# Attention and ternary FFN on one core: scores made twice instead of transposing p, and one written schedule of 64 heads

## The chip, the cores and the metric

The kernel runs on one core of a Trainium2 chip. The metric is the device time of one execution, in microseconds (us). The kernel before takes 694.51 us, the median of three runs (694.48 to 696.26).

PE is the tensor engine (PEld its weight loads), DVE the vector engine, ACT the scalar engine, POOL GpSimd, SP the engine that issues most DMAs. Each runs its own program in order, and they meet by semaphores.

## The reference, cut to what matters

```python
# x: (4, 512, 512) f32; 16 query heads of 32, one key and one value head
q = rotary((x @ Wq + bq).reshape(4, 512, 16, 32).transpose(0, 2, 1, 3))
k = rotary((x @ Wk + bk)[:, None])
v = (x @ Wv + bv)[:, None]
scores = einsum('bhqd,bhkd->bhqk', q, k) / sqrt(32)
attn = softmax(scores, axis=-1)
ctx = einsum('bhqk,bhkd->bhqd', attn, v)            # -> (4, 512, 512)
x = layernorm(x + ctx @ Wo + bo)
# FFN: w1, w2 (1408, 512), w3 (512, 1408); ternary weights
qz = lambda w: clip(round(w / (mean(abs(w)) + 1e-8)), -1, 1)
hidden = sigmoid(x @ qz(w1).T) * (x @ qz(w2).T)
out = layernorm(x + hidden @ qz(w3).T)
```

## The kernel before, in words

Four batches of 512 tokens are worked one after another. A batch has 16 heads, in four groups of four. Queries are projected per group (a unit, `q0` to `q3`, f32 products, eight instructions), keys once (unit `k`). A unit is copied out of its bank by ACT into `raw`, rotated by POOL (times cosine) and DVE (shuffle, times sine, sum), and split into a high and a low half in the matmul's reduced f32 type, `hi` and `lo`. SP then stacks the four heads of a unit into `q_st` by 16 small DMAs (`stack`), high and low on different partitions, so that one product of 128 rows gives a score of f32 quality against `k_st`.

For each head and each tile t of 128 queries:

1. `score` (PE, L935): one product 128x128 by 512 keys into a ring of three banks `s_ps`, in the first batch four.
2. `row_max` (DVE, L697): the minimum of the negated scores, straight from the bank.
3. `exps` (ACT, L458): the exponential with that shift as bias; `accum_out` sums the row. p stands by query.
4. `turn` (PE, L947): 16 transposes of 128x128 per head bring p to stand by key, into two banks `t_ps`; ACT and DVE each `move` two of the four tiles to `pt_sb` (L468, L703).
5. After four heads, `context` (PE, L997): the values' 32 columns against `pt_sb`, the heads in four column strips of the array, each k tile of each head two instructions. The reciprocals of the sums are spread and turned (`reciprocals`, `turn_sums`, `norm_row`), and DVE multiplies (`normalise`).

Beside the heads of batch b runs the output projection (`wo0` to `wo3`), the layer norm, the turning of h (`ht`) and the FFN (`up`, 11 tiles of two halves, `dn0` to `dn3`) of batch b - 1, in banks `a_ps` and `b_ps`, placed by a list:

```python
BESIDE = (["up0", "up1", "up2", "up3", "q2", "up4", "up5", "up6", "q3"]
          + [f"up{f}" for f in range(7, FT)] + ["dn0", "dn1", "dn2", "dn3"])
```

wo and ht stand ahead of the batch's heads, with `q0`, `k` and `q1`. The first batch has heads only (`first_heads`), and there ACT sums the absolute weights, DVE rounds w1 and w3 (`quantise`) and POOL w2 (`round_w2`). Batches 1 to 3 are one loop body of each engine. After it comes a tail: wo, ht, up and dn of batch 3 alone. The order of each engine's work is written out by hand in `first_heads`, `heads` and `period`; no planner is used.

## Time and profile before

| | |
|---|---|
| median of the runs | 694.51 us |
| the profiled execution | 694.24 us |
| its span, first to last instruction | 692.4 us |
| PE busy | 634.5 us (92%) |
| DVE busy | 491.6 us (71%) |
| ACT busy | 353.3 us (51%) |
| POOL busy | 93.1 us (13%) |
| mean granted clock of PE | 0.968 |

Busy PE is not PE at its peak: products are pipelined and their shown ends overlap the next start. How long one takes in a row of many is read from the distance of starts. The profile's page names lines of the kernel before (L955 is `turn`, L944 `score`, L916 `up`, L930 `dn`, L882 a query unit, L903 `wo`, L1008 `context`, L962 the key and value parts, L893 `ht`).

### The profile page before, as it was taken

How to read it: one execution, taken by the hardware profiler on the slowest of the kernel's cores; microseconds unless marked ns; L12 is line 12 of the kernel's file. 1: busy time of each engine (PE TensorE's matmuls, PEld its weight loads, DVE VectorE, ACT ScalarE, POOL GpSimd, SP SyncE). 2: the span in 40 equal slices, each digit the busy share in tenths (PEclk: the TensorE clock that was granted, in tenths of full speed). 3: DMA queues.
4: the chain of work that ended last, by engine and by line, in shares of the span. 5: the costliest groups of instructions: out<-in, count | busy, mean ns of one | idle time of the engine just before them, and what ended most of it. 6: DMA issues, size and time to landing. Idle time of an engine off the chain costs nothing.

```text
span 692.4 us, 10936 instructions
## 1 busy us (share of the span) xinstructions
PE 634.5 (92%) x3342; PEld 347.6 (50%) x3342; DVE 491.6 (71%) x833; ACT 353.3 (51%) x814; POOL 93.1 (13%) x118
## 2 busy tenths in 40 slices
PE   6777577699999999999999999999999999998996
PEld 2544345434556565634556565534556564543442
DVE  2879967947887985758887985658878985554333
ACT  2795576522676585412677685312767675302320
POOL 1000562012000400121000400122000400110001
PEclk9799789799999999999999999999999999999999
DMA  7662450001132040021122030011122110000001
GB/s 268 228 204 62 167 162 22 1 16 46 29 95 62 9 114 3 16 65 46 43 85 58 23 101 2 25 61 41 47 88 51 29 34 2 31 30 1 0 1 61
DMA packets 20516, 42.03 MB, mean 61 GB/s; under 512 B 4704, under 2 KB 5856, under 8 KB 19936
## 3 DMA queue, kind: packets, MB, share of 16 engines
q1 hardware_dynamic: 19488, 39.86, 19.0%
q10 hardware_dynamic: 960, 1.33, 0.5%
q8 instruction: 34, 0.56, 0.3%
q14 instruction: 34, 0.28, 0.1%
HBM read 20.20 MB, written 4.19 MB: 35 GB/s over the span
## 4 chain that ended last, share of the span: by engine, by line
PE 74%; DVE 11%; issue 6%; ACT 3%; DMA 3%; SPq 1%; POOL 1%; DVEq 0%; POOLq 0%; ACTq 0%
PE t_ps L955 14%; PE a_ps L916 11%; PE b_ps L916 10%; PE c_ps L1008 8%; PE a_ps L882 7%; PE s_ps L944 6%; PE a_ps L930 6%; PE b_ps L930 6%; PE a_ps L903 3%; DVE sh_sb L700 3%; DMA late<-in_w 2%; PE b_ps L903 2%; DVE pt_sb L707 1%; SPq L286 1%; PE a_ps L993 1%
## 5 line engine op out<-in xcount | busy, mean ns | idle before, releaser
L464 ACT ACTIVATE p_sb<-s_ps,sh_sb 128x512 f32<-128x512 f32 x240 | 164.4, 689 | 106.9 <-DVE sh_sb L700 106.9
L955 PE MATMUL t_ps<-table_sb,p_sb 128*128 128x128 f32 x1024 | 143.5, 284 | 26.4 <-ACT pt_sb L472 23.7
L700 DVE TENSOR_REDUCE sh_sb<-s_ps 128x1 f32<-128x512 f32 x240 | 157.6, 679 | 0.8 <-PE s_ps L944 0.7
L955 PEld LDWEIGHTS t_ps<-table_sb,p_sb 128*128 128x128 f32 x1024 | 123.0, 146 | 67.0 <-ACT p_sb L464 33.3
L707 DVE COPY pt_sb<-t_ps 128x512 f32<-128x512 f32 x128 | 88.1, 688 | 69.3 <-PE t_ps L955 67.5
L472 ACT ACTIVATE pt_sb<-t_ps 128x512 f32<-128x512 f32 x128 | 76.5, 597 | 51.4 <-PE t_ps L955 49.6
L944 PE MATMUL s_ps<-k_st,q_st 128*128 128x512 f32 x240 | 91.0, 463 | 4.0 <-DVE k_st L627 2.5
L916 PE MATMUL a_ps<-late,q 128*128 128x512 f16 x352 | 85.2, 386 | 3.5 <-DVE late L642 3.4
L916 PE MATMUL b_ps<-late,q 128*128 128x512 f16 x352 | 83.6, 380 | 0.0
L882 PE MATMUL a_ps<-xT_sb,wq_sb 128*128 128x512 f32 x128 | 61.8, 614 | 8.7 <-DMA wq_sb<-in_wq 6.4
L361 POOL TENSOR_TENSOR rot<-raw,table_sb 128x512 f32<-128x512 f32 x20 | 25.9, 1295 | 306.6 <-ACT raw L433 291.6
L1008 PE MATMUL c_ps<-pt_sb,v_sb 128*32 128x512 f32 x512 | 59.5, 606 | 2.1 <-DVE pt_sb L707 2.1
L916 PEld LDWEIGHTS a_ps<-late,q 128*128 128x128 f16 x352 | 32.0, 99 | 46.9 <-issue 8.2
L916 PEld LDWEIGHTS b_ps<-late,q 128*128 128x128 f16 x352 | 31.9, 98 | 39.4 <-issue 5.4
L944 PEld LDWEIGHTS s_ps<-k_st,q_st 128*128 128x128 f32 x240 | 43.1, 200 | 12.1 <-ACT p_sb L464 5.8
L464 ACT ACTIVATION_READ_ACCUMULATOR p_sb<-s_ps,sh_sb 128x1 f32 x240 | 48.3, 201 | 0.0
L377 POOL TENSOR_SCALAR rstd<-mv 128x1 f32<-128x1 f32 x32 | 8.4, 263 | 278.0 <-DVE mv L670 277.9
L930 PE MATMUL b_ps<-q,late 128*128 128x512 f16 x176 | 41.3, 380 | 0.0
L903 PE MATMUL a_ps<-wo_sb,cx 128*128 128x512 f32 x88 | 40.2, 599 | 0.5 <-DVE late L690 0.4
L930 PE MATMUL a_ps<-q,late 128*128 128x512 f16 x176 | 40.4, 380 | 0.0
L882 PEld LDWEIGHTS a_ps<-xT_sb,wq_sb 128*128 128x128 f32 x128 | 23.3, 195 | 33.0 <-issue 23.9
L657 DVE SCALAR_TENSOR_TENSOR b_ps<-th,b_ps 128x512 f32<-128x512 f32 x33 | 23.0, 696 | 22.6 <-PE b_ps L916 20.5
(82 smaller groups left out, 602.2 us busy)
## 6 DMA issues: line engine op xcount, KB each, us to landing
q_st<-hi SPq DMA_DIRECT2D x128, 64.0 KB, 2.0
q_st<-lo SPq DMA_DIRECT2D x128, 64.0 KB, 2.0
late<-in_w SPq DMA_DIRECT2D x2, 2816.0 KB, 11.3
xT_sb<-in_xT SPq DMA_DIRECT2D x8, 512.0 KB, 4.9
late<-in_x SPq DMA_DIRECT2D x4, 1024.0 KB, 5.6
out<-late SPq DMA_DIRECT2D x16, 256.0 KB, 2.0
late<-in_w SPq DMA_DIRECT2D x2, 1408.0 KB, 6.9
wo_sb<-in_wo SPq DMA_DIRECT2D x1, 1024.0 KB, 5.6
```

Of the source, the lines that this page charges most:

```text
L361: pool.tensor_tensor(rot[:, 0, :], raw[:, u % 2, :], cos_sb, ALU.mult).then_inc(cos_done, 1)
L464: act.activation(p_sb[:, h % 2, t, :], score_bank(b, n), ACT.Exp, bias=sh_sb[:, n % (2 * SR):n % (2 * SR) + 1], scale=-1.0, accum_out=sums ...
L472: act.activation(pt_sb[:, h % PTR, k, :], t_ps[k % 2][:, :], ACT.Copy).then_inc(pt_act, 1)
L700: dve.tensor_reduce(sh_sb[:, n % (2 * SR):n % (2 * SR) + 1], score_bank(b, n), AX.X, ALU.min).then_inc(maxed, 1)
L707: dve.tensor_copy(pt_sb[:, h % PTR, k, :], t_ps[k % 2][:, :]).then_inc(pt_dve, 1)
L882: mm = pe.matmul(a_ps[:, :], wq_sb[:, k, g * P:(g + 1) * P], xT_sb[:, k, :], start=(k == 0), stop=(k == DT - 1))
L903: mm = pe.matmul(ps[:, :], cx[:, g, t * P:(t + 1) * P], wo_sb[:, g, :], start=(g == 0), stop=(g == HG - 1))
L916: mm = pe.matmul(ps[:, :], w[:, k, f * P:(f + 1) * P], hT[:, s, k, :], start=(k == 0 and s == 0), stop=(k == DT - 1 and s == 1))
L930: mm = pe.matmul(ps[:, :], gT[:, s, f, t * P:(t + 1) * P], q3v[:, f, :], start=(f == 0 and s == 0), stop=(f == FT - 1 and s == 1))
L944: pe.matmul(score_bank(b, n), q_st[:, h % (QR * HPG), t * P:(t + 1) * P], k_st[:, :], start=True, stop=True).then_inc(scored, 1)
L955: mm = pe.transpose(t_ps[k % 2][:, t * P:(t + 1) * P], p_sb[:, h % 2, t, k * P:(k + 1) * P], id_sb)
L1008: mm = pe.matmul(c_ps[HD * j:HD * (j + 1), :], v_sb[:, k, :], pt_sb[:, (g * HPG + j) % PTR, k, :], start=(k == 0), stop=(k == TT - 1))
```

## The change

The scores are made twice. `rows` is the old `score`, used only for the maximum of each query; `cols` takes `k_st` as the weights and `q_st` as the moving side, so the scores stand by key. In front of a group of four heads DVE spreads the maxima (high and low part, `spread_maxima`), PE turns them (`turn_maxima`), ACT copies them to `mrow`, and four `pick` products per head, 32 rows of the array each, subtract the query's maximum inside the bank. ACT's exponential then writes `pt_sb` directly, without bias and without a row sum. The 16 transposes of p per head, their moves and `p_sb` are gone.

The sums of p over the keys are made by PE with a matrix of ones: for the first two groups (DIRECT) from the four k tiles of p, later from `acc`, into which POOL has added the four tiles (`add_keys`, three additions per head). DVE inverts them with its own transposes of 32x32 (`inverse_sums`).

Banks: four `t_ps`, one for each k tile of `cols`; `a`, `b`; `c` for key, value and context; `r` for `rows`, the turned maxima and the sums. Up to head 21 the `rows` alternate between `r` and `b`, after it all are in `r`.

All three steps of a rotation are on POOL, and so is all rounding of weights. ACT waits, before it copies the key or value parts of the next batch into `lo`, until all four units of the batch have been stacked. The order is one list of slots, one slot a head, straight through all 64 heads, with no loop body; `rows` run four heads ahead of `cols`, and every engine follows the same `order`. wo, ht, up of batch b - 1 start at slot 3, its last two down tiles stand in slots 1 and 2 of batch b + 1. The first units are made key first.

```diff
-PTR = HPG
-PIECES = 8
-W2_PIECES = 4
-SR = 3
-UNITS = ["q0", "k", "q1", "q2", "q3"]
+N = B * H
+PTR = HPG + 1
+PIECES = 4
+DIRECT = 2
+TWO_BANKS = 22
+UNITS = ["k", "q0", "q1", "q2", "q3"]
+BESIDE = [
+    ["ctx3a", "ctx3b", "q2a", "q2b"],
+    ["sums3", "dn2a", "dn2b", "dn2c"],
+    ["dn3a", "dn3b", "dn3c"],
+    ["wo0a", "wo0b", "wo1a", "wo1b"],
+    ["ctx0a", "ctx0b", "wo2a", "wo2b"],
+    ["sums0", "wo3a", "wo3b", "q3a", "q3b"],
+    ["ht0", "ht1", "ht2", "ht3"],
+    ["up0a", "kp", "up0b", "key", "up1a"],
+    ["vp", "up1b", "val", "up2a", "ctx1a", "ctx1b"],
+    ["sums1", "up2b", "up3a", "up3b", "q0a"],
+    ["q0b", "up4a", "up4b", "up5a"],
+    ["up5b", "up6a", "up6b", "up7a"],
+    ["ctx2a", "ctx2b", "up7b", "up8a"],
+    ["sums2", "up8b", "q1a", "q1b", "up9a"],
+    ["up9b", "up10a", "up10b", "dn0a"],
+    ["dn0b", "dn0c", "dn1a", "dn1b", "dn1c"],
+]
+FIRST = [
+    ["q2a", "q2b"], ["tot0"], [], [],
+    ["ctx0a", "ctx0b", "sums0"], ["tot1", "q3a", "q3b"], [], ["kp", "key", "vp", "val"],
+    ["ctx1a", "ctx1b", "sums1"], ["q0a", "q0b"], [], [],
+    ["ctx2a", "ctx2b"], ["sums2", "q1a", "q1b"], ["tot2"], [],
+]
+OPENING = ["kp", "q0a", "q0b", "key", "vp", "q1a", "val", "q1b"]
...
+def order(b, h):
+    if b >= B:
+        return chunks(b, h)
+    beside, names = chunks(b, h), []
+    if h % HPG == 0:
+        names += ["turn"] + beside[:1]
+        beside = beside[1:]
+    names += ["cols"]
+    for t in range(TT):
+        if b * H + h + HPG < N:
+            names += [f"rows{t}"]
+        names += beside[t:t + 1]
+    return names + beside[TT:]
+def row_bank(n, t):
+    return "rb"[t % 2] if n < TWO_BANKS else "r"
...
 @block.sync
+            def stack(b, g):
+                sp.wait_ge(hi_done, unit(b, f"q{g}") + 1)
+                for j in range(HPG):
+                    n = b * H + g * HPG + j
+                    if n >= QR * HPG:
+                        sp.wait_ge(cols_filled, n - QR * HPG + 1)
+                    for r in (0, 2, 1, 3):
+                        half = (hi, lo)[r % 2]
+                        if j == 0 and r == 1:
+                            sp.wait_ge(lo_done, unit(b, f"q{g}") + 1)
+                        sp.dma_start(q_st[HD * r:HD * (r + 1), ring(n), :].bitcast(F32),
+                                     half[HD * j:HD * (j + 1), :].bitcast(F32)).then_inc(q_in[j], 16)
+            for b in range(B):
+                if b >= 2:
+                    store(b - 2, 0)
+                    store(b - 2, 1)
+                stack(b, 2)
+                if b >= 2:
+                    store(b - 2, 2)
+                    store(b - 2, 3)
+                if b + 1 < B:
+                    load_xT(b + 1)
+                stack(b, 3)
+                if b == 0:
+                    sp.wait_ge(rounded, PIECES)
+                    sp.dma_start(stage[2], w3).then_inc(w_ffn[2], 16)
+                load_x(b)
+                if b + 1 < B:
+                    stack(b + 1, 0)
+                    stack(b + 1, 1)
+            for c in (B - 2, B - 1):
+                for t in range(TT):
...
 @block.gpsimd
+            def rotate(b, name):
+                u = unit(b, name)
+                where = "c" if name == "k" else "a"
+                pool.wait_ge(drained[where], at("key" if name == "k" else name, b))
+                pool.wait_ge(rotated, u)
+                pool.tensor_tensor(rot[:, 0, :], raw[:, :], cos_sb, ALU.mult).then_inc(cos_done, 1)
+                pool.wait_ge(swapped, u + 1)
+                pool.tensor_tensor(rot[:, 1, :], rot[:, 1, :], sin_sb, ALU.mult).then_inc(sin_done, 1)
+                pool.wait_ge(sin_done, u + 1)
+                pool.wait_ge(cos_done, u + 1)
+                pool.tensor_tensor(rot[:, 1, :], rot[:, 0, :], rot[:, 1, :], ALU.add).then_inc(rotated, 1)
+            def add_keys(n, step):
+                j, p, done = n % HPG, n % PTR, 3 * (n - DIRECT * HPG)
+                if step == 0 and n // HPG > DIRECT:
+                    pool.wait_ge(filled["r"], at(f"sums{(n // HPG - 1) % HG}", (n // HPG - 1) // HG))
+                pool.wait_ge(expd, n * TT + step + 2)
+                if step:
+                    pool.wait_ge(added, done + step)
+                pool.tensor_tensor(acc[:, j, :], acc[:, j, :] if step else pt_sb[:, p, 0, :],
+                                   pt_sb[:, p, step + 1, :], ALU.add).then_inc(added, 1)
...
 @block.scalar
+            def take_parts(b, name):
+                act.wait_ge(filled["c"], at(name, b))
+                for j in range(HPG):
+                    act.wait_ge(q_in[j], b * HG * 16 * 4)
+                act.activation(part[:, :], c_ps[:, :], ACT.Copy).then_inc(drained["c"], 1)
+            def take_maxima(gg):
+                act.wait_ge(filled["r"], at("turn", gg, "r"))
+                act.activation(mrow[:, :], r_ps[:, :], ACT.Copy).then_inc(drained["r"], 1)
+            def exps(n, k):
+                act.wait_ge(cols_filled, n + 1)
+                if k == 0 and n >= PTR:
+                    old = n - PTR
+                    gg = old // HPG
+                    act.wait_ge(filled["c"], at(f"ctx{gg % HG}", gg // HG))
+                    if gg < DIRECT:
+                        act.wait_ge(filled["r"], at(f"sums{gg % HG}", gg // HG))
+                    else:
+                        act.wait_ge(added, 3 * (old - DIRECT * HPG + 1))
+                act.activation(pt_sb[:, n % PTR, k, :], t_ps[k][:, :], ACT.Exp).then_inc(expd, 1)
...
 @block.vector
+            def row_max(n, t):
+                where = row_bank(n, t)
+                dve.wait_ge(filled[where], at(f"rows{t}", n, where))
+                dve.tensor_reduce(mx[:, t, n % HPG:n % HPG + 1], banks[where][:, :], AX.X,
+                                  ALU.max).then_inc(drained[where], 1)
+            def spread_maxima(gg):
+                last = gg * HPG + HPG - 1
+                for t in (TT - 2, TT - 1):
+                    where = row_bank(last, t)
+                    dve.wait_ge(drained[where], at(f"rows{t}", last, where))
+                if gg == 0:
+                    dve.wait_ge(turned_set, 1)
+                else:
+                    dve.wait_ge(filled["r"], at("turn", gg - 1, "r"))
+                every = mx[:, :, :].unsqueeze(2).broadcast_to([P, TT, HPG, HPG])
+                dve.tensor_copy(maxima[:, :, :, 0:HPG], every).then_inc(max_hi, 1)
+                dve.wait_ge(max_hi, gg + 1)
+                dve.tensor_tensor(maxima[:, :, :, HPG:2 * HPG], every, maxima[:, :, :, 0:HPG].bitcast(F32),
+                                  ALU.subtract).then_inc(max_done, 1)
+            def inverse_sums(gg):
+                name, b = f"sums{gg % HG}", gg // HG
+                dve.wait_ge(filled["r"], at(name, b))
+                dve.tensor_reduce(sm[:, :], r_ps[:, :].rearrange("p (m r) -> p m r", r=HD), AX.X, ALU.max,
+                                  apply_transpose=True).then_inc(drained["r"], 1)
+                dve.wait_ge(drained["r"], at(name, b))
+                dve.reciprocal(rc[:, :], sm[:, :]).then_inc(recip_done, 1)
+                dve.wait_ge(recip_done, gg + 1)
+                dve.transpose(rT.rearrange("p (m r) -> p m r", r=HD),
+                              rc[:, :].unsqueeze(2).broadcast_to([P, TT * HPG, HD])).then_inc(rT_done, 1)
+            def follow(b, name):
+                if name[:2] == "up" and name[-1] == "b":
+                    g_low(batch_of(b, name), int(name[2:-1]))
+                elif name[:4] == "sums":
+                    normalise(batch_of(b, name) * HG + int(name[4]))
+            def end(b, name):
+                if name[:2] == "wo" and name[-1] == "b":
+                    norm(batch_of(b, name), 0, int(name[2]))
+                elif name[:2] == "dn" and name[-1] == "c":
+                    norm(batch_of(b, name), 1, int(name[2]))
+                for name in order(b, h):
+                    chunk(b, h, name)
+                    follow(*gone[-1])
+                    end(*gone[-3])
+                    stack_halves(*gone[-5])
+                    gone.append((b, name))
...
 @block.tensor
+            def rows(n, t):
+                b, h = divmod(n, H)
+                where = row_bank(n, t)
+                ps = start_bank(f"rows{t}", n, where)
+                if t == 0:
+                    pe.wait_ge(q_in[n % HPG], (n // HPG + 1) * 16 * 4)
+                if t == 0 and h == 0:
+                    pe.wait_ge(lo_done, unit(b, "k") + 1)
+                pe.matmul(ps[:, :], q_st[:, ring(n), t * P:(t + 1) * P], k_st[:, b % 2, :],
+                          start=True, stop=True).then_inc(filled[where], 1)
+            def turn_maxima(gg):
+                start_bank("turn", gg, "r")
+                pe.wait_ge(max_done, gg + 1)
+                for t in range(TT):
+                    mm = pe.transpose(r_ps[:, t * P:(t + 1) * P], turned[:, t, :].bitcast(F32), id_sb)
+                mm.then_inc(filled["r"], 1)
+            def cols(n):
+                b, j = n // H, n % HPG
+                if n == 0:
+                    pe.wait_ge(pick_set, 1)
+                if j == 0:
+                    pe.wait_ge(drained["r"], at("turn", n // HPG, "r"))
+                for k in range(TT):
+                    if n:
+                        pe.wait_ge(expd, (n - 1) * TT + k + 1)
+                    pe.matmul(t_ps[k][:, :], k_st[:, b % 2, k * P:(k + 1) * P], q_st[:, ring(n), :],
+                              start=True, stop=False)
+                for k in range(TT):
+                    mm = pe.matmul(t_ps[k][:, :], pick[HD * k:HD * (k + 1), j, :], mrow[HD * k:HD * (k + 1), :],
+                                   start=False, stop=True)
+                mm.then_inc(cols_filled, 1)
+            def sums(gg):
+                start_bank(f"sums{gg % HG}", gg // HG)
+                if gg < DIRECT:
+                    pe.wait_ge(expd, (gg + 1) * HPG * TT)
+                    for k in range(TT):
+                        for j in range(HPG):
+                            mm = pe.matmul(r_ps[HD * j:HD * (j + 1), :], ones[:, 0:HD],
+                                           pt_sb[:, (gg * HPG + j) % PTR, k, :], start=(k == 0), stop=(k == TT - 1))
+                else:
+                    pe.wait_ge(added, 3 * HPG * (gg - DIRECT + 1))
+                    for j in range(HPG):
+                        mm = pe.matmul(r_ps[HD * j:HD * (j + 1), :], ones[:, 0:HD], acc[:, j, :],
+                                       start=True, stop=True)
+                mm.then_inc(filled["r"], 1)
```

## Rows read from the trace of the kernel before

**Rows 1.** Stretches: us; PE, PEld, DVE, ACT, POOL busy; granted clock, DMA share, GB/s.

```profile
21.80:144.57 122.77, 88.84 (x487) 57.78 (x487) 100.49 (x167) 80.72 (x190) 25.74 (x18) 0.85 0.35 115
...
456.80:607.60 150.80, 149.61 (x829) 82.30 (x828) 113.28 (x193) 83.98 (x197) 17.82 (x23) 1.00 0.15 42
607.60:692.40 84.80, 75.08 (x313) 33.78 (x311) 36.46 (x64) 15.88 (x26) 7.66 (x18) 0.96 0.05 19
```

**Rows 2.** Timeline of PE, a head beside an up tile: start, us, instruction.

```profile
337.96 0.93 PE L944 MATMUL s_ps<-k_st,q_st 128*128 128x512 f32 x3
338.74 1.90 PE L916 MATMUL a_ps<-late,q 128*128 128x512 f16 x8
340.48 1.04 PE L955 MATMUL t_ps<-table_sb,p_sb 128*128 128x128 f32 x8
341.27 0.50 PE L944 MATMUL s_ps<-k_st,q_st 128*128 128x512 f32 x1
341.62 1.90 PE L916 MATMUL b_ps<-late,q 128*128 128x512 f16 x8
```

**Rows 3.** Timeline of PE, key parts and what follows.

```profile
148.20 1.06 PE L962 MATMUL c_ps<-xT_sb,small_sb 128*32 128x512 f32 x8
149.19 3.70 PE L903 MATMUL a_ps<-wo_sb,cx 128*128 128x512 f32 x8
```

**Rows 4.** Groups by line: count, busy us, mean ns, idle before and its releaser.

```profile
L700 DVE TENSOR_REDUCE sh_sb<-s_ps 128x1 f32<-128x512 f32 x240 | 157.6, 679 | 0.8 <-PE s_ps L944 0.7
...
L707 DVE COPY pt_sb<-t_ps 128x512 f32<-128x512 f32 x128 | 88.1, 688 | 69.3 <-PE t_ps L955 67.5
L472 ACT ACTIVATE pt_sb<-t_ps 128x512 f32<-128x512 f32 x128 | 76.5, 597 | 51.4 <-PE t_ps L955 49.6
```

**Rows 5.** Timeline: a lone score and its row maximum, and a last DVE step of ht.

```profile
484.37 0.58 PE L944 MATMUL s_ps<-k_st,q_st 128*128 128x512 f32 x1
...
485.17 0.68 DVE L700 TENSOR_REDUCE sh_sb<-s_ps 128x1 f32<-128x512 f32 x1
...
626.81 0.69 DVE L642 SCALAR_TENSOR_TENSOR late<-b_ps,late 128x512 f16<-128x512 f32 x1 [0.30 <-ACT late L440]
```

**Rows 6.** Timeline of the opening: stacking, splitting and rotating.

```profile
15.89 1.23 SPq L286 DMA_DIRECT2D q_st<-hi  x2
...
18.37 0.69 DVE L617 TENSOR_TENSOR rot<-rot 128x512 f32<-128x512 f32 x1
...
19.09 0.42 DVE L624 CAST k_st<-rot 64x512 fp32r<-64x512 f32 x1
19.35 1.28 POOL L361 TENSOR_TENSOR rot<-raw,table_sb 128x512 f32<-128x512 f32 x1 [1.62 <-ACT raw L433]
19.54 1.37 DVE L625 CAST k_st<-rot 64x512 fp32r<-64x512 f32 x1
```

**Rows 7.** The chain that ended last, in order of time: w2's load, a context.

```profile
26.66 13.15 DMA late<-in_w
...
235.10 3.57 PE c_ps L1008 x32
```

**Rows 8.** Waits from 22 to 144.57: us in total, times, longest.

```profile
PE t_ps L955 <- ACT pt_sb L472: 23.7, 15, 3.9
```

**Rows 9.** Waits of PE from 144.57 to 609: us in total, times, longest.

```profile
PE a_ps L882 <- issue: 2.0, 2, 1.3
PE a_ps L916 <- DVE late L642: 2.0, 3, 0.7
PE a_ps L903 <- DVE late L690: 0.4, 2, 0.3
```

**Rows 10.** Timeline of PE in the tail: the last wo to the first up.

```profile
617.89 3.60 PE L903 MATMUL b_ps<-wo_sb,cx 128*128 128x512 f32 x8
621.32 0.60 PE L893 MATMUL a_ps<-table_sb,late 128*128 128x128 f32 x4
...
627.56 3.55 PE L916 MATMUL a_ps<-late,q 128*128 128x512 f16 x8 [1.42 <-DVE late L642]
```

More of the change, by code:

```diff
@@ L1124, in _ @@
[L1124 to L1138 removed]
+                if third == 2:
+                    mm.then_inc(filled[where], 1)
```

1245 lines of the change are left out of this document (466 added, 779 removed).

## The prediction

> **What bounds the kernel now.** I read the table of stretches first. It cuts the span where PE begins a new batch. In the three middle periods (144.57 to 607.60, on average 154.3 us) PE is busy nearly all the time at full clock, DVE about 75% and ACT 56% (here of the last one). In the first batch (21.8 to 144.57) PE is busy 72%, the granted clock falls to 0.85 and a head takes 122.8 / 16 = 7.7 us; DVE is the fullest engine [rows 1]. The timeline of PE in a middle period says how full it really is: the starts of the groups follow each other with no gap, 8 transposes 0.79 us, 3 scores 0.78 (0.26 each), 8 f16 products of 512 columns 1.74, a score alone 0.35 [rows 2]. The longer groups: key parts (four column strips at once) 0.99 [rows 3], a context of four heads 3.57 [rows 7], a four-tile f32 product, eight instructions, 3.43 [rows 10]. Added up over a period (64 scores, 256 transposes, 4 contexts, 11 up pairs, 4 down, 8 f32 products, small ones) this gives about 150 of 154.3 us. So the middle is PE's, by issued work; only in the first batch do the others decide. There the waits say who: PE for ACT's move of the transposed tile, 23.7 us [rows 8].
>
> The chip must therefore be asked two things: does PE get less work per batch, and does the new order keep PE fed.
>
> **PE's work per period.** Removed: 16 transposes per head, two groups of 0.79, so 16 x 1.58 = 25.3 us, and the four turns of sums at 0.4, 1.6 us; together 26.9. Added:
> - `cols`, four scores by key, 4 x 0.26 = 1.05 per head [rows 2]: 16.8.
> - the four `pick` products that add the maximum. Each has 32 rows of the array and 512 columns. No row shows row strips. Upper bound: each costs a score, 4 x 0.26 = 1.05 per head. Lower bound: all four stream as one, 0.26. The nearest row is the key parts, where 8 instructions on four column strips take 0.99, while two instructions of the four-tile product take 3.43 / 4 = 0.86 [rows 3, 10], so strips run together; with four weight loads I take 0.45: 7.2.
> - `rows` is today's score, but now always alone: 48 of them rise from 0.26 to 0.32: 2.9.
> - turning the maxima, 4 x 0.42 (half a group of eight): 1.7; `sums` as four column strips, 4 x 1.0: 4.0.
>
> Added 32.6, net +5.7 us per period. The work that leaves ACT (two moves of 597 ns) and DVE (two moves of 688 ns) [rows 4] is worth nothing here, because PE did not wait for them.
>
> Of the pick products the Trainium skill says more ("TensorE: Matmul & The Clock Gate", section "Measured speedup vs the span model"): four tiles of 32 rows and 512 columns ran 3.07 times as fast as one after another. By that rule a head would pay 1.05 / 3.07 = 0.34 and the period 1.8 us less than in my sum; no row here shows it.
>
> **New waits of PE.** From head 22 on, `rows` has the single bank `r`. A lone score's row maximum starts 0.80 us after the row says the score started (0.6 after it really streams, behind the previous group), the reduction takes 0.68 [rows 4, 5], and PE goes on 0.06 after a DVE end (626.81 + 0.69 against 627.56) [rows 5, 10], say 0.1. So from a `rows` to the next use of `r` about 0.6 + 0.68 + 0.1, 1.35 us, of which 0.3 is its own: PE needs 1.05 us of other work between. Most chunks are halves of 1.72 and hide it, with 0.7 left for one DVE operation ahead in its queue. Where they don't:
> - `sums0` to `sums3` also use `r` and stand directly between `rows0` and `rows1`: 1.05 before, 1.05 after (a reduction again), four times: 8.4.
> - slot 6 puts the four `ht` (0.42 each) between the `rows`. Each has an ACT copy and a DVE subtraction in front of the next row maximum, and ACT has two exponentials first, and the split of q3 stands in DVE's queue. Worked through, the slot takes 6.9 us after `cols` for 2.9 us of work: 4.0.
> - after wo0, wo2, dn3 and dn0 the evacuation with its statistics (1.6 us of DVE) stands before a row maximum: four times 0.7, 2.8.
> - `kp` of the next batch must be copied into `lo`, so ACT waits until SP has issued all 16 copies of q3: 0.63 us each [rows 6], 10.1, which end about 2 us after PE wants `key`: 2.0.
>
> Together 17.2. Today's waits, 4.4 us over three periods [rows 9], may go: -1.5. The period becomes 154.3 + 5.7 + 17.2 - 1.5 = 175.7 us.
>
> Work also moves between stretches. Of what three periods hold today, the new ones lack two down tiles (9.5), one batch's q0, q1 and key and value parts (10.7) and `rows` of four heads (5.1), which stand in front or behind: 3 x 175.7 - 25.3 = 501.8 us against 463.0: +38.8.
>
> **Opening and first batch.** Today the first score stands at 21.8 [rows 1]. Now the order is: key first (its three rotation steps now on POOL at 1.28 each instead of one there and two of 0.69 on DVE [rows 6]), so q0's halves about 27 instead of 15.9; 16 copies at 0.63 and 2.0 landing: 39.6; DVE's q1 split waits for them in front of the maxima of heads 2 and 3, eight at 0.60 follow; turning: first `cols` at 46.
> A bare slot is a loop: `cols` end, 0.25, four exponentials at 0.60 (as long as ACT's move of a bank [rows 4]), the last bank's score 0.26, picks 0.45: 3.6 us, where a head had 7.7. That is the gain of the change: 16 x 3.6 = 57.6. On top comes what stands in one line with it: three contexts 10.7, sums directly from p (two at 3.57, then 1.0) 8.1, four q units 13.7, key and value chunks 3.8, maxima 2, the wait for w2 (its load goes out only after q1's copies, about 50; today it went at 26.66 and took 13.15 [rows 7]) 2. And `kp` at slot 7 meets q3's copies: q3b, 0.9 ACT, 4.0 POOL, 1.1 DVE, 10.1 SP, 2.0 landing, against 7.7 of PE work: 10.7. POOL, with eight roundings of 4.6 us and three additions per head from head 8 on, holds the split of q0 (3) and `sums2` (4.5). Sum 116, end at 162 us, against 144.6 today: +17.4.
> The additions of p for three quarters of the heads are 3 x 1.28 = 3.9 us per head on POOL, under a slot of 10.9; hidden outside this stretch.
>
> **Tail.** Today 84.8 us [rows 1]. New in it: context of the last group 3.6, its sums 1.0 and their wait for POOL 0.7, two down tiles of batch 2, 2 x 4.75, and norm three names after wo, so that ht2 and ht3 come later: today 6.2 us lie between the end of the last wo (621.32) and the first up [rows 10], then about 8.2. Together 16.8, so 101.6. The up pairs stay at 1.73 per product: th now carries the gate too, and the loop gate, g_high, g_low, tanh ends 3.3 us after the product that starts it, just under two products.
>
> **Sum.** 692.4 + 17.4 + 38.8 + 16.8 = 765.4 us of span. The profiled execution took 694.24 with a span of 692.4, 1.8 more, and the median of the runs, 694.51, is 0.3 above it. So 767 us.
>
> **Rivals.**
> - It is faster. Mechanism: neither the bank `r` nor the copies of q3 hold PE, because DVE and ACT have more air than I give them, so the bare loop of 3.6 us per head decides in the first batch. Place: the 17.2 us of waits per period and the 18.2 in the first batch go (51.6 + 18.2), and picks cost 0.34 (7): 767 - 77 = 690. If also the opening, where I let every step wait for the last, is 5 us shorter, 685. It decides once less than about 5 of these 82 us remain, since the sum without them is 9 below today. For it: ACT drops from 51% to a third; DVE rows are short [rows 4]. Against: a `sums` between two `rows` on one bank can't be hidden by idle engines, it is latency. Chance 0.12.
> - The pick products run one after another (no strips by rows): 0.6 more per head, 64 heads, +38: 805 us. For it: no row shows it otherwise. Chance 0.10.
> - DVE and POOL hold each other up. While POOL multiplied at 19.35, a DVE cast that takes 0.42 took 1.37 [rows 6]. POOL now works half of each period instead of an eighth, and g_low reads th and gT in SBUF instead of a bank. Some 34 DVE operations per batch read SBUF (g_low, halves, swap, norm); half of them meet POOL at 0.95 each, 16 us per period, of which half lies in front of a row maximum or a gate: 3 x 8, 791 us. Chance 0.10. By the Trainium skill ("SBUF — State Buffer", section "Who interferes with whom") a DVE operation with two SBUF inputs, or in a two-port mode, and a GpSimd operation that reads SBUF exclude each other for a whole instruction; the row agrees.
> - The gains of the first batch and the losses balance, 692 to 697: 0.03.
>
> **Numbers.** The forecast, 767, has 0.65; its own range is 728 to 800 (first batch 20 either way, waits of a period 6 either way, picks 0.26 to 0.6). Range over the cases: 705 to 803; below lies most of the faster case, above half of the serial picks. A change under 0.3% is what this kernel's measurement can't tell from none. Faster 0.12, same 0.03, slower 0.85.
>
> **What would show it.** The starts of `cols`, pick and `rows` give their spacing: 0.26, 0.45 per four, 0.3. Idle of PE before `sums` and before the `rows1` behind it, 1 us each, released by DVE's row maximum and by the transposing reduction. Slot 6: `rows` released by DVE. First `cols` near 46, b=1 beginning near 162, batch periods near 176, the tail 102. PE's idle before `key`, released by ACT, 10 us in the first batch. I am wrong if PE's idle time in the middle is under 5 us per period, or if the first batch ends before 140.

## The result and the profile after

The changed kernel takes 837.06 us (median of 4 runs, 834.47 to 837.82) against 695.12 for the kernel before on the same chip: ratio 1.202, 95% interval 1.198 to 1.206. It is 142 us slower. The forecast, 767, had the direction right and the size wrong: 837 lies outside the range of 705 to 803.

The page's busy times and its slices (tenths of 40 equal slices) show no full engine:

```profile
PE 683.8 (82%) x3006; PEld 302.5 (36%) x3006; DVE 442.3 (53%) x682; ACT 239.5 (29%) x430; POOL 396.0 (48%) x351
...
PE   5478758768877898888987798988987999987997
...
POOL 2325465798946329255546328255546282531001
PEclk9678969788889899999999999999999999998999
```

The table of stretches of the kernel after, cut at its first `cols`, at the turn of the maxima of each new batch and at the last context (columns as in [rows 1]):

```profile
0.00:51.00 51.00, 28.22 (x66) 11.68 (x67) 19.38 (x33) 7.95 (x12) 12.59 (x16) 0.77 0.49 159
51.00:185.11 134.11, 97.03 (x434) 41.98 (x433) 73.73 (x115) 52.65 (x94) 82.13 (x62) 0.86 0.30 96
185.11:379.17 194.06, 162.93 (x694) 72.05 (x695) 106.43 (x156) 55.35 (x101) 111.40 (x92) 0.91 0.13 35
379.17:567.36 188.19, 160.60 (x739) 72.16 (x738) 112.32 (x168) 55.37 (x101) 93.60 (x83) 0.98 0.14 40
567.36:726.91 159.55, 143.90 (x681) 64.86 (x679) 87.79 (x135) 52.34 (x96) 82.18 (x74) 0.98 0.09 27
726.91:832.70 105.79, 91.09 (x397) 39.80 (x396) 42.64 (x75) 15.88 (x26) 14.07 (x25) 0.94 0.05 20
```

Against [rows 1]: a middle period had 1.2 us of TensorE's idle time, now b=1 and b=2 have 31 and 28. In b=1 the granted clock is 0.91, and TensorE is busy 162.9 us with less work than in b=2, where it is busy 160.6 at 0.98: so its own products take longer there as well. Set beside the forecast the span's 67.3 us too many (832.7 against 765.4) fall so: opening 51.0 for 46 (+5.0), first batch 134.1 for 116 (+18.1), b=1 194.1 for 166.2 (+27.9), b=2 188.2 for 175.7 (+12.5), b=3 159.6 for 159.9 (-0.4), tail 105.8 for 101.6 (+4.2). (The forecast's 166.2 and 159.9 are its 175.7 less the 9.5, and less the 10.7 and 5.1, that it let move out of these batches.)

What TensorE waited for, over the whole span (us in total, times, longest):

```profile
PE r_ps L842 <- DVE mx L631: 56.0, 51, 3.4
PE r_ps L849 <- DVE turned L647: 16.0, 9, 3.5
PE c_ps L825 <- ACT lo L494: 12.1, 3, 9.8
PE r_ps L842 <- DVE sm L653: 10.5, 13, 0.8
PE r_ps L891 <- DVE mx L631: 9.4, 12, 0.8
...
PE b_ps L842 <- DVE mx L631: 6.9, 9, 1.7
PE r_ps L891 <- POOL acc L399: 3.4, 1, 3.4
```

L842 is `rows`, L849 the turn of the maxima, L825 the key's product, L891 the sums. The forecast had the third to fifth lines. The first two, 72 us, it had only in a few places.

Where do they come from? The timeline of all engines at one such wait, in b=2:

```profile
506.75 1.77 DVE L715 TENSOR_TENSOR late<-th,late 128x512 f16<-128x512 f32 x1
...
507.94 6.04 POOL L426 TENSOR_TENSOR late<-late,b_sb 128x512 f32<-128x512 f32 x4
...
508.45 1.50 DVE L617 CAST hi<-rot 128x512 fp32r<-128x512 f32 x1
...
508.60 0.50 PE L842 MATMUL r_ps<-k_st,q_st 128*128 128x512 f32 x1
...
509.98 1.64 DVE L619 TENSOR_TENSOR lo<-rot,hi 128x512 fp32r<-128x512 f32 x1
...
511.54 0.68 DVE L631 TENSOR_REDUCE mx<-r_ps 128x1 f32<-128x512 f32 x1
...
512.27 0.50 PE L842 MATMUL r_ps<-k_st,q_st 128*128 128x512 f32 x1 [1.43 <-DVE mx L631]
```

The score at 508.60 ends about 509.0, its maximum is taken at 511.54, because the cast and the subtraction of the next query unit stand ahead in DVE's queue, at 1.50 and 1.64 us while POOL works in SBUF beside them. TensorE gets bank `r` back at 512.27. It had 1.9 us of other work and would have needed 3.3. POOL's work at this place is the adding of `bo` (L426), which the kernel before has too; elsewhere it is the new additions of p, the rotations or the rounding of weights.

The groups of DVE show that these operations in SBUF are longer on the mean of the whole kernel, and others with them. After:

```profile
L715 DVE TENSOR_TENSOR late<-th,late 128x512 f16<-128x512 f32 x44 | 39.7, 903 | 15.1 <-ACT late L529 13.4
...
L680 DVE TENSOR_SCALAR late<-late,mv,rstd 128x512 f32<-128x512 f32 x32 | 26.4, 824 | 8.2 <-POOL rstd L420 8.2
L619 DVE TENSOR_TENSOR lo<-rot,hi 128x512 fp32r<-128x512 f32 x16 | 24.7, 1541 | 0.5
...
L617 DVE CAST hi<-rot 128x512 fp32r<-128x512 f32 x16 | 15.9, 994 | 5.8 <-POOL rot L389 5.0 <-DMA q_st<-lo 0.8
...
L645 DVE CAST turned<-mx 128x64 fp32r<-128x64 f32 x16 | 8.3, 517 | 1.4
L647 DVE TENSOR_TENSOR turned<-mx,turned 128x64 fp32r<-128x64 f32 x16 | 7.9, 496 | 0.5
```

The same operations in the kernel before:

```profile
L674 DVE TENSOR_SCALAR late<-late,mv,rstd 128x512 f32<-128x512 f32 x32 | 17.0, 532 | 6.3 <-POOL rstd L380 6.2
...
L635 DVE TENSOR_TENSOR lo<-rot,hi 128x512 fp32r<-128x512 f32 x16 | 12.1, 757 | 0.6
L633 DVE CAST hi<-rot 128x512 fp32r<-128x512 f32 x16 | 11.1, 695 | 1.0 <-DVE rot L617 0.9
```

The row maximum itself, which reads a PSUM bank, is as long as before (684 ns here, 679 in [rows 4]).

### The profile page after: what moved, and what is told of

The parts are those of the page before. It is cut to its first block and busy times, and to the rows that moved or that the text cites. A ratio compares the mean times of both kernels' runs of the same rounds, so it can differ in the third digit from the quotient of the medians.

```text
span 832.7 us, 8501 instructions
## 1 busy us (share of the span) xinstructions
PE 683.8 (82%) x3006; PEld 302.5 (36%) x3006; DVE 442.3 (53%) x682; ACT 239.5 (29%) x430; POOL 396.0 (48%) x351
## 3 DMA queue, kind: packets, MB, share of 16 engines
q10 hardware_dynamic: 960, 1.33, 0.4%
## 5 line engine op out<-in xcount | busy, mean ns | idle before, releaser
L631 DVE TENSOR_REDUCE mx<-r_ps 128x1 f32<-128x512 f32 x212 | 144.9, 684 | 145.4 <-PE r_ps L842 144.2
L842 PE MATMUL r_ps<-k_st,q_st 128*128 128x512 f32 x212 | 125.6, 592 | 74.7 <-DVE mx L631 56.0
L510 ACT ACTIVATE pt_sb<-t_ps 128x512 f32<-128x512 f32 x256 | 136.3, 600 | 171.2 <-PE t_ps L864 165.5
L399 POOL TENSOR_TENSOR acc<-acc,pt_sb 128x512 f32<-128x512 f32 x112 | 145.4, 1299 | 18.6 <-ACT pt_sb L510 4.3
L399 POOL TENSOR_TENSOR acc<-pt_sb 128x512 f32<-128x512 f32 x56 | 74.3, 1326 | 92.8 <-PE r_ps L891 91.3
L842 PEld LDWEIGHTS r_ps<-k_st,q_st 128*128 128x128 f32 x212 | 42.1, 199 | 146.4 <-DVE mx L631 83.0
L861 PE MATMUL t_ps<-q_st,k_st 128*128 128x512 f32 x256 | 82.0, 444 | 0.2 <-ACT pt_sb L510 0.2
L861 PEld LDWEIGHTS t_ps<-q_st,k_st 128*128 128x128 f32 x256 | 50.4, 203 | 31.2 <-issue 16.7
L710 DVE SCALAR_TENSOR_TENSOR th<-th,b_ps 128x512 f32<-128x512 f32 x44 | 30.2, 686 | 50.9 <-PE b_ps L931 50.3
L715 DVE TENSOR_TENSOR late<-th,late 128x512 f16<-128x512 f32 x44 | 39.7, 903 | 15.1 <-ACT late L529 13.4
```

The costliest lines, as they stand in the source:

```text
L399: pool.tensor_tensor(acc[:, j, :], acc[:, j, :] if step else pt_sb[:, p, 0, :], pt_sb[:, p, step + 1, :], ALU.add).then_inc(added, 1)
L510: act.activation(pt_sb[:, n % PTR, k, :], t_ps[k][:, :], ACT.Exp).then_inc(expd, 1)
L631: dve.tensor_reduce(mx[:, t, n % HPG:n % HPG + 1], banks[where][:, :], AX.X, ALU.max).then_inc(drained[where], 1)
L710: dve.scalar_tensor_tensor(out=th[:, :], in0=th[:, :], scalar=1.0, in1=b_ps[:, :], op0=ALU.add, op1=ALU.mult).then_inc(drained["b"], 1)
L715: dve.tensor_tensor(gT[:, 1, f, :], th[:, :], gT[:, 0, f, :], ALU.subtract).then_inc(g_low_done, 1)
L842: pe.matmul(ps[:, :], q_st[:, ring(n), t * P:(t + 1) * P], k_st[:, b % 2, :], start=True, stop=True).then_inc(filled[where], 1)
```

## The experiments

Theories. **W**: one bank `r` for rows, turns and sums, emptied by DVE; what TensorE waits for is that round trip. **P**: POOL's additions lengthen DVE's operations in SBUF that stand ahead of it. **C**: idling lowers TensorE's clock, a cost of its own. **G**: TensorE's issued work sets the time. Each run is compared with the changed kernel's 837.06. A gain's interval is about 3 us either way (ratios of each run to the kernel before have half-widths of 0.3 to 0.4%).

**The additions shortened.**

```diff
-                pool.tensor_tensor(acc[:, j, :], acc[:, j, :] if step else pt_sb[:, p, 0, :],
-                                   pt_sb[:, p, step + 1, :], ALU.add).then_inc(added, 1)
+                pool.tensor_tensor(acc[:, j, 0:8], acc[:, j, 0:8] if step else pt_sb[:, p, 0, 0:8],
+                                   pt_sb[:, p, step + 1, 0:8], ALU.add).then_inc(added, 1)
```

> Leaves out most of POOL's additions: each takes 8 of the 512 columns of p, so acc is not the sum. Same order, same semaphores. Changed kernel: 837 us, span 832.7. Theory W (PE waits for DVE through the single bank r; POOL lengthens DVE's operations on SBUF only as a second cause): the split of q falls from 0.99 and 1.54 us to 0.43 and 0.69, g_low from 0.90 to 0.68, norm from 0.82 to 0.53, and the waits that are above the predicted ones (10 us in the third batch, as much or more in the first two) go: about 25 us less, 812. Rival P (the additions on POOL are the main cause): 60 us or more, at or under 777. Rival G (the work that PE issues is the cause): within 8 us of 837.

Measured 801.7 us (800.1 to 804.9), -35.4. The groups of DVE in this run:

```profile
L716 DVE TENSOR_TENSOR late<-th,late 128x512 f16<-128x512 f32 x44 | 31.1, 706 | 19.0 <-ACT late L530 17.1
...
L681 DVE TENSOR_SCALAR late<-late,mv,rstd 128x512 f32<-128x512 f32 x32 | 18.4, 576 | 6.0 <-POOL rstd L420 5.7
L620 DVE TENSOR_TENSOR lo<-rot,hi 128x512 fp32r<-128x512 f32 x16 | 17.2, 1076 | 0.6
...
L618 DVE CAST hi<-rot 128x512 fp32r<-128x512 f32 x16 | 9.6, 599 | 5.8 <-POOL rot L389 5.0 <-DMA q_st<-lo 0.8
```

The waits of `rows` for a maximum in bank `r` fell from 56.0 to 34.9 us. What the additions cost by this run is 35 us; neither theory had the number (W said 25, P 60 or more), and G's 8 fell. POOL's own lateness is a small part of it: TensorE's wait for `acc` goes from 3.4 to 0.2 us, ACT's from 5.7 to nothing. The subtraction for `lo` stays at 1076 ns, where the kernel before had 757: POOL still has the rotations and the rounding that the change moved to it, and what those cost was not tried. The two profiled spans are 29.6 apart (832.7 and 803.1). By the turns of the maxima at 183.21, 362.88 and 543.88 that falls so: the first batch, whose additions begin only at head 8, 1.9; b=1 14.4 (194.1 to 179.7, of which 5.8 is shorter busy time of TensorE, at a clock of 0.95 for 0.91); b=2 7.2 (188.2 to 181.0); the rest 6.1.

**The row maximum shortened.**

```diff
-                dve.tensor_reduce(mx[:, t, n % HPG:n % HPG + 1], banks[where][:, :], AX.X,
+                dve.tensor_reduce(mx[:, t, n % HPG:n % HPG + 1], banks[where][:, 0:64], AX.X,
```

> Leaves out most of the row maximum: it reduces 64 of the 512 keys, so the maximum subtracted is only that of these. The products rows stay. Theory W: a wait on the bank r is 0.68 of reduction out of about 1.35 us; at 0.2 us each of some 80 waits loses about 0.5, and DVE's queue gets 256 x 0.48 = 120 us of air: 45 to 60 us less, about 785. Rival G: PE's issued work decides, under 15 us less, over 822. Rival P: the long DVE operations stay as they are beside POOL, and the waits behind them too: about 810.

Measured 807.7 (805.4 to 809.5), -29.4: nearer to P's number (810) than to W's (785), so the reduction's own 0.68 us is only a part of the round trip. The waits of `rows` fell to 47.0, those of the sums for a maximum from 9.4 to 3.8, those of the turns from 16.0 to 10.1. The gain is 10 us in the first batch (b=1 begins at 175.15), 5 in b=1 and 6 in b=2.

**The sums ahead of `cols`** (sums1 to sums3, so that `cols`, not a `rows` that needs the same bank, stands behind them).

```diff
+    elif beside and beside[0] in ("sums1", "sums2", "sums3"):
+        names += beside[:1]
+        beside = beside[1:]
     names += ["cols"]
```

> One edit to the order: sums1, sums2 and sums3 stand ahead of cols instead of between rows0 and rows1; sums0 stays, since its normalisation waits for wo3. Theory W: in front of each PE idled 0.79 us and behind it 0.84; cols covers the first from the other side, and for 9 of the groups both go: about 15 us less, 822; the waits released by the transposing reduction fall from 13 to 4 or 5. Rival G or P: no more than 5 us less.

Measured 827.8 (825.9 to 832.1), -9.3, between W's 15 and the 5 at most of the others; the waits behind the sums fell from 10.5 to 4.2 us. This edit loses nothing of the computation, as the next.

**The key's parts later in the first batch.**

```diff
-    [...], [...], [], ["kp", "key", "vp", "val"],
-    ["ctx1a", "ctx1b", "sums1"], ["q0a", "q0b"], [], [],
+    [...], [...], [], [],
+    ["ctx1a", "ctx1b", "sums1", "kp", "key"], ["vp", "q0a", "val", "q0b"], [], [],
```

> In the first batch alone the key and value parts of the next batch move from slot 7 to slots 8 and 9. Theory W: the 9.8 us wait of PE for ACT's copy into lo, which waits for the copies of q3, goes, and with it the low granted clock behind it (products of cols at 0.38 instead of 0.26 for some 10 us): 10 to 14 us less, about 824. Rival: the time is bound by POOL in this stretch anyway (rounding, then additions), and it comes back before sums2: under 4 us less.

Measured 830.1 (828.6 to 831.6), -6.9. The key's product in the first batch, first in the changed kernel, then in this run:

```profile
111.36 2.08 PE L825 MATMUL c_ps<-lo,table_sb 128*128 128x512 f32 x2 [9.84 <-ACT lo L494]
```

```profile
120.47 1.13 PE L825 MATMUL c_ps<-lo,table_sb 128*128 128x512 f32 x2 [0.29 <-ACT lo L494]
```

The wait of 9.84 is gone, the gain is 6.9, between W's 10 to 14 and the rival's under 4: a wait of 5.9 on `rows` that wasn't there stands in the first batch instead.

**All four.**

> The four edits of e1 to e4 together: POOL adds 8 of 512 columns of a head's exponentials (the sums are of part of them), the row maxima are taken over 64 of 512 keys, sums1 to sums3 stand ahead of cols, and the key's parts and product move to slot 8. Alone they gave -35.4, -29.4, -9.3 and -6.9 us, 81 together. If they are separate causes (each step's own wait), the time is 837 - 81 = 756, within 6. If the additions act by lengthening the very row maxima and copies that e2 shortens (mutual hold-up of DVE and POOL is the one cause behind both), the parts overlap and it is 770 to 785. If what is left is TensorE's own issued work, whose busy time was 684 of 832, it can't come below about 740.

Measured 754.7 (752.4 to 757.5), -82.4, where the four alone sum to 81.0. The gains add up as the theory of separate causes said; the 770 to 785 of one shared cause is not met. By the two profiled spans, 80.5 apart, 61 us of it are idle time of TensorE (148.9 to 88.0) and 20 its busy time, which falls from 683.8 to 664.2 with the same products, at a granted clock of 0.948 for 0.926. TensorE is now busy 88% of its span; the two middle periods between the turns at 168.47, 332.74 and 500.33 last 164.3 and 167.6.

**No pick products.** The exponentials are of the bare scores; the banks are ended by the score by key.

```diff
-                    pe.matmul(t_ps[k][:, :], ..., start=True, stop=False)
-                for k in range(TT):
-                    mm = pe.matmul(t_ps[k][:, :], pick[HD * k:HD * (k + 1), j, :], mrow[HD * k:HD * (k + 1), :],
-                                   start=False, stop=True)
+                    mm = pe.matmul(t_ps[k][:, :], ..., start=True, stop=True)
```

> Leaves out the four products of each head that add minus the maximum (the exponentials are of the bare scores). Theory that TensorE's issued work is on the path: 64 x 0.44 = 28 us go, 809. Theory that the engine waits for the maxima's copies and reductions anyhow (they are still waited for, since the turn of the maxima and its bank are kept): a part of the 28 turns into longer waits for row maxima, and 10 to 20 us go, 817 to 827. If picks were made one after another rather than together, 64 x 1.05 = 67 us would go, 770.

Measured 820.3 (816.5 to 825.2), -16.8. The waits of `rows` for a maximum in `r` grew from 56.0 to 63.1. The other theory's 10 to 20 us is met, but waits are only half of the reason: TensorE's idle time grows by 9 us (148.9 to 158.0), and its busy time falls by 18.4 (683.8 to 665.4) and not by 28, at a granted clock of 0.896 for 0.926. With less to do TensorE got a lower clock, and the products that were left took longer.

> e5 (755 us) without the four products that add minus the maximum. Theory that e5 has only TensorE's issued work on the path: 64 x 0.44 = 28 us go, 727. In the changed kernel itself (e6) only 17 went, since waits filled the place. If waits still set the pace in e5: 735 to 745.

The same edit on the kernel of all four: 730.1 (729.1 to 731.2), -24.5 from 754.7. That is near the 28 of issued work. It isn't that fewer waits swallow it: TensorE's idle time grows by 17 here (88.0 to 104.8), more than the 9 in the run before. But the granted clock holds, 0.951 for 0.948, where it fell there. No run holds the clock fixed, so this share is read from the profiles and not shown.

**Rows on 8 keys.** The scores by query are made, and their maxima taken, on 8 of the 512 keys.

```diff
-                pe.matmul(ps[:, :], q_st[:, ring(n), t * P:(t + 1) * P], k_st[:, b % 2, :],
+                pe.matmul(ps[:, 0:8], q_st[:, ring(n), t * P:(t + 1) * P], k_st[:, b % 2, 0:8],
```

> The scores by query are made and their maxima taken on 8 of the 512 keys only: the second making of the scores and most of the reduction go, all waits and copies stay. Of this e2 gave 29 us with 64 columns. 256 products at 0.26 to 0.34 us that shrink to some 0.06 are 50 to 70 us of TensorE's work more. Theory that TensorE is then still the bound: 837 - 29 - 60 = 748, range 735 to 760. Theory that DVE and POOL with their mutual hold-up set the pace by then (DVE was busy 442, POOL 396 of 832): over 770.

Measured 776.0 (774.5 to 777.5), -61.1; less 29.4 of e2 this is 31.7 for the products. TensorE still waits 45.9 us for maxima that now take 0.16 us each: so the wait is for the queue ahead of the maximum, not for the maximum itself. G's 748 was too low, the other theory's "over 770" is met. The granted clock is 0.905, where e2 had 0.925. An 8-column product beside others still holds TensorE for 0.13 to 0.22 us, by the starts behind it in this run, not the 0.06 expected:

```profile
470.79 0.27 PE L842 MATMUL r_ps<-k_st,q_st 128*128 128x8 f32 x1
470.93 1.90 PE L931 MATMUL b_ps<-late,q 128*128 128x512 f16 x8
```

> e5 (755 us) with the scores by query made, and their maxima taken, on 8 of 512 keys. What TensorE gives up per product is 0.34 less what an 8-column product takes with its weight load: e7 against e2 gave 32 us for 256 of them, 0.12 each. Theory that e5 is bound by TensorE's issued work alone: more goes than in e7, 256 x 0.12 to 0.24 = 32 to 60 us, 695 to 723. Theory that something else bounds it: over 735.

On the kernel of all four: 730.0 (728.7 to 732.3), -24.6. Neither theory's figure (695 to 723, or over 735). TensorE's idle time grows from 88.0 to 103.4 us and its clock falls from 0.948 to 0.925, so a part of the work saved comes back as waits and as longer products.

**TensorE kept busy.** 68 products that nothing reads, at the places of its long waits.

```diff
+            def junk(n, count):
+                pe.wait_ge(expd, (n - 1) * TT + 1)
+                for _ in range(count):
+                    pe.matmul(t_ps[0][:, :], k_st[:, 0, 0:P], k_st[:, 0, :], start=True, stop=True)
...
+                if 1 <= gg <= 5:
+                    junk(gg * HPG, 6)
```

> TensorE makes products of no use into t_ps0 where it idled longest: 6 ahead of each turn of the maxima in groups 1 to 5, 7 before the row product behind slots 11 and 15, and 24 ahead of the key of batch 1; 68 products of about 0.22 to 0.43 us, most of them inside waits of 2 to 10 us. Theory that the low granted clock of the first 380 us (0.77, 0.86 and 0.91 in the first three stretches, where the kernel before had 0.968 over all) is a cause by itself, fed by the idling: the granted clock of these stretches rises to 0.95 or more and 15 to 25 us go, 812 to 822. Theory that the clock follows from the waits and costs little: within 4 us of 837, or up to 10 slower where the products outlast the waits.

Measured 826.6 (825.5 to 827.4), -10.5. The stretch 45 to 180 in the changed kernel and in this run:

```profile
45.00:180.00 135.00, 100.27 (x440) 43.73 (x439) 71.05 (x115) 53.24 (x95) 77.39 (x58) 0.85 0.30 97
```

```profile
45.00:180.00 135.00, 111.52 (x527) 53.92 (x527) 75.02 (x120) 53.88 (x96) 83.85 (x63) 0.97 0.32 102
```

The granted clock rose from 0.85 to 0.97 there, and 10.5 us went though work was added. That lies between the two theories, 15 to 25 and 4 at most: the clock is a cost of its own, as C says, but this run gives back less than expected, about 8 us of it in the first batch (b=1 begins at 176.96 for 185.11). From 180 to 370 the clock rose from 0.90 to 0.94 and b=1 lasted 191.9 for 194.1.

**The additions in the kernel before.** Three for each of the first 12 heads of a batch, of constant tables.

```diff
+                for h in range(first_head, first_head + 4):
+                    pool.wait_ge(expd, (b * H + h) * TT + 1)
...
+                    for i in range(3):
...
+                        pool.tensor_tensor(spare[:, :], cos_sb, sin_sb, ALU.add).then_inc(spare_done, 1)
```

> The kernel before, with three additions of 128x512 on POOL behind each of the first 12 heads of a batch (144 in all, of constant tables into a tile that nothing reads), as the changed kernel has 168. Theory that the additions hold DVE up whatever the kernel: DVE's subtractions with two inputs in SBUF go from about 0.7 to 1.4 us and the time rises by 10 to 25 us, to 705 to 720. Theory that the hold-up costs much only where one bank r passes every score row, sum and turn through DVE's queue: the subtractions lengthen as much, but the time rises by less than 5 us, under 700.

Measured 708.4 (707.7 to 709.9) against 695.9, ratio 1.0193 (1.0168 to 1.0219), +12.6. The key parts that begin the periods, in this run:

```profile
158.35 1.07 PE L979 MATMUL c_ps<-xT_sb,small_sb 128*32 128x512 f32 x8
...
313.68 1.06 PE L979 MATMUL c_ps<-xT_sb,small_sb 128*32 128x512 f32 x8
...
469.21 1.06 PE L979 MATMUL c_ps<-xT_sb,small_sb 128*32 128x512 f32 x8
```

In the kernel before the first of these stands at 148.20 [rows 3], the next two here:

```profile
303.23 1.06 PE L962 MATMUL c_ps<-xT_sb,small_sb 128*32 128x512 f32 x8
...
457.51 1.07 PE L962 MATMUL c_ps<-xT_sb,small_sb 128*32 128x512 f32 x8
```

The rise is clear of the noise and inside the 10 to 25 us of the first theory; the second theory's "less than 5" fell. 10.2 of the 12.6 us arise in the first batch, where DVE is the fullest engine: there it rounds weights in SBUF, and the two roundings went from 1006 to 1421 and from 576 to 859 ns, 16 of each, 11 us together. The changed kernel has that work on POOL. The next two periods last 155.3 and 155.5 us with the additions, 155.0 and 154.3 without. But hardly anything was lengthened in them: DVE's busy time grows by 1.4 us a period, where the additions of the changed kernel add 12.6 to b=1 and 13.9 to b=2 (against e1). The subtraction for `lo` rose from 757 to 1053 ns on the mean, to 1541 in the changed kernel; the 128x512 f16 result reads a bank here and stayed at 682 ns, there it reads `th` in SBUF and takes 903. So the run shows that the additions lengthen DVE's work in SBUF in another kernel too. Whether such a lengthening is cheap where TensorE is full, and dear only behind the one bank `r`, it does not settle.

**No additions, sums by TensorE.**

```diff
-DIRECT = 2
+DIRECT = 16
```

> The changed kernel with all 16 groups summed by TensorE directly, as groups 0 and 1 are, and no additions on POOL; nothing is left out. A group's sums rise from 1.2 to 3.65 us of TensorE, 14 x 2.45 = 34 us more; the additions' cost goes, which e1 measured at 35. Theory that both hold: within 6 us of 837. Theory that the additions cost more than e1 showed (it kept their issue and their semaphores): under 828. Theory that TensorE isn't the bound where the sums stand: under 820.

Measured 835.1 (834.1 to 839.1), -1.9: 29.7 us more of TensorE's busy time (713.5 for 683.8) pay for what the additions cost. That is inside the first theory's 6 us. The waits of `rows` for a maximum in `r` are 37.7 us here, much as in e1 (34.9), for 56.0: so it is the additions and not the loss of their result that e1 shows. POOL's additions bought nothing in the changed kernel. No version ran faster than the kernel before.

## Why the prediction was wrong, step by step

**Right.** TensorE bounded the middle of the kernel before, so the moves taken from ACT and DVE bought nothing. In the changed kernel's bare slots, the timeline of PE:

```profile
62.80 1.09 PE L861 MATMUL t_ps<-q_st,k_st 128*128 128x512 f32 x4
63.82 0.51 PE L864 MATMUL t_ps<-mrow,pick 32*128 32x512 f32 x4
64.25 0.50 PE L842 MATMUL r_ps<-k_st,q_st 128*128 128x512 f32 x1
64.59 0.40 PE L842 MATMUL b_ps<-k_st,q_st 128*128 128x512 f32 x1
65.54 0.50 PE L842 MATMUL r_ps<-k_st,q_st 128*128 128x512 f32 x1 [0.55 <-DVE mx L631]
```

Four `cols` take 1.02 us (1.05 said), four picks 0.43 (0.45 said), a lone row 0.34 (0.32 said). Serial picks are refuted. The Trainium skill's factor ("TensorE: Matmul & The Clock Gate", section "Measured speedup vs the span model") would give 0.34; this trace gives 1.02 / 0.43 = 2.4 times, not 3.07. The issued work per period was sound too, where the clock is full: in b=2 of the kernel of all four TensorE is busy 157.6 of 167.6 us at a clock of 0.99, in b=2 of the changed kernel 160.6 at 0.98, where I had 175.7 - 17.2 = 158.5. The wait for sums was foreseen at 1.05 ahead and 1.05 behind and is 0.8 either way (9.4 us over 12 and 10.5 over 13). The wait for `key` was foreseen at 10.7 and is 9.84.

**Wrong, the term "new waits of PE", 17.2 us per period.** As the views of waits add up it was 34.5 in b=1 (31.1 of idle time), 27.6 in b=2 and 15.7 in b=3. Behind it stand two mis-sizings, and beside it in b=1 a term that I put at nothing, the clock.

*DVE's queue ahead of a maximum.* I took each DVE operation at its length in the kernel before, gave half chunks "0.7 left for one DVE operation ahead", and listed only the exceptions of sums, slot 6, the evacuations and `key`. Beside POOL that operation takes up to 1.6 us, and for each query unit there are two of them in a row. This was my rival of DVE and POOL, at 0.10 and 24 us; e1 measured 35, of which 21.6 in b=1 and b=2 alone, and e10, which leaves nothing out, agrees. The mechanism should have been in the forecast itself: [rows 6] had shown 0.42 become 1.37, and the change puts 3.9 us per head on POOL. By the Trainium skill ("SBUF — State Buffer", section "Who interferes with whom") the two exclude each other for whole instructions; the means of `lo` (757 to 1541 ns) and the unchanged row maximum from PSUM (684) agree with it.

*The round trip of bank `r` where nothing stands beside the rows.* b=1 has no down tiles, and I booked them at -9.5 us. But their absence leaves slots of bare rows, each of which pays the round trip. The price of one use was right, 1.35 us foreseen; what was wrong is "most chunks are halves of 1.72 and hide it", since slot 1 of b=1 has only the sums and slot 2 nothing beside its rows. The slot at 205 in b=1, 7.87 us long:

```profile
205.21 1.91 PE L861 MATMUL t_ps<-q_st,k_st 128*128 128x512 f32 x4
207.05 0.80 PE L864 MATMUL t_ps<-mrow,pick 32*128 32x512 f32 x4
208.60 0.49 PE L842 MATMUL r_ps<-k_st,q_st 128*128 128x512 f32 x1 [0.76 <-DVE mx L631]
209.88 0.50 PE L842 MATMUL r_ps<-k_st,q_st 128*128 128x512 f32 x1 [0.78 <-DVE mx L631]
211.16 0.54 PE L842 MATMUL r_ps<-k_st,q_st 128*128 128x512 f32 x1 [0.78 <-DVE mx L631]
212.49 0.80 PE L842 MATMUL r_ps<-k_st,q_st 128*128 128x512 f32 x1 [0.78 <-DVE mx L631]
```

Rows stand 1.28 to 1.33 us apart where 0.34 is their work, and the row maximum between them is not lengthened. That the down tiles' absence is worth less than their work, the batch lengths show: on the kernel of all four b=1 is 164.3 and b=2 167.6, 3.3 apart and not 9.5; in the changed kernel, at the lower clock, b=1 is even 5.9 longer. b=3, which has no query unit and no key of a next batch to split in DVE's queue, came out as forecast (159.6); that its missing splits are the reason is argued and was not tried (its own q2 and q3 are still split in it).

*The clock.* The sum takes every product at the price it has at full clock. b=1 had 0.91, and TensorE was busy 162.9 us for the 149.0 that the forecast leaves it (158.5 less the 9.5): of the 27.9 us that b=1 was too long 13.9 are this, as much as the waits above the forecast (31.1 for 17.2). In the kernel of all four, at 0.97, b=1 is busy 152.1. In b=2 the two shares of the 12.5 us are 2.1 (busy time) and 10.4 (idle time).

**Wrong, the first batch (116 us; 134.1).** A bare slot was to take 3.6 us. It took 3.7 where nothing else came in (62.80 to 66.47), but only there: with a unit's halves in DVE's queue 5.2 (57.65 to 62.80, a wait of 1.61 behind a maximum). e2 gave 10 us here, keeping TensorE busy 8, the later key 6 (b=1 began at 179.09); these need not add. The clock was no term of mine here either, though the first batch before had 0.85 [rows 1].

**Wrong, turning the maxima.** I had its product (0.42) and, for the maxima, 2 us in the first batch. TensorE waits 16.0 us at it, nine times, for two copies of 128x64 that take 0.5 us each beside POOL. The kernel of all four still has 11.1 of it.

**Small.** The opening was 5 us longer than said and the tail 4.2; no experiment was made on either. Neither sign that I gave of being wrong came (idle time in the middle under 5 us per period, a first batch that ends before 140): both looked only for a kernel faster than forecast.

**Where the expected 767 and the measured 837 part.** Of the 142 us lost to the kernel before, 82.4 are in the four places of e1 to e4. The forecast had 51.6 us of waits in the periods and 18.2 in the first batch, 70 together, but at the sums, slot 6, the evacuations and the key; e3 and e4, which take away only nine of the waits at the sums and the one at the key of the first batch, gave 16. The queue ahead of the maxima (e1, e2: 65) is what it left out. The 59 us that e5 still stands above the kernel before hold the added work (picks 24.5, most of the second scores 24.6, against the transposes that went), the opening and tail, and waits such as the 20.8 us for maxima and 11.1 at the turns that e5 shows; how these share it out was not taken further, and the losses at slot 6 and after the evacuations were not tried by themselves. Nor were two changes that would test the causes from the other side: a second bank for `rows` beyond head 21, and the two steps of each rotation that moved to POOL back on DVE.

## What to carry to other kernels

When a change gives an idle engine a long run of SBUF work, reprice every SBUF operation of its neighbour, and then every short wait behind that neighbour's queue: the sum of work was right here to 2 us in a period at full clock, the waits were off by up to a factor of two. DVE operations that read a bank kept their length here, so a result that is moved from a bank to SBUF pays too. And where new waits come in, count the clock as well: in b=1 it cost as much as the waits above the forecast. A single buffer bank between two engines costs its whole round trip, queue included, at each use that has less other work beside it. Work that "goes away" from a slot shortens it only if nothing else in that slot was hidden under it.

## What the runs showed of the hardware that was not expected

- Additions of 128x512 on POOL cost 12.6 us in one kernel (144 of them) and 35.4 in the other (168). They lengthen DVE's operations in SBUF in both, but DVE's busy time grows by 16 us in the first (491.6 to 507.8) and by 38 in the second (403.8 to 442.3).
- In the kernel before with additions the `hi` cast went the other way, from 695 to 487 ns on the mean, while `lo` rose from 757 to 1053: which operations meet POOL seems a matter of when they fall; it was not traced.
- Small operations suffer as well: the copy of the maxima, 128x64, takes 517 ns beside the additions and 337 in e1.
- Useless products in TensorE's waits raised the granted clock of 135 us from 0.85 to 0.97 and made the kernel 10.5 us faster.
- Less work for TensorE came with a lower granted clock: without the picks 0.896 for 0.926, with rows on 8 keys 0.905 for 0.925 and 0.925 for 0.948. With more work it rose (sums by TensorE, 0.939 for 0.926). Only without the picks in the kernel of all four did it stay (0.951 for 0.948).
- A product with 8 moving columns instead of 512 saved only 0.10 to 0.12 us on the path (24.6 and 31.7 us over 256), where a full one takes 0.34. It still holds TensorE for 0.13 to 0.22 us, and its weight load shows 0.19; the rest went into waits and the clock.
